# Self-attention on one core: the projection matmuls dealt out over the head slots

## What is computed

```python
x = x + attn(layernorm(x), w_qkv, w_out)      # 16 heads of 32, causal
x = x + xattn(layernorm(x), ctx, ctx, wq, wk, wv, wo)
x = x + ffn(layernorm(x), wg, W, b)           # top-1 of 8 experts
# attn: q, k, v = split(x @ w_qkv); p = softmax(mask(q k^T / sqrt(32))); (p v) @ w_out
```

## Time and profile before

| | us |
|---|---|
| median of 3 runs | 864.57 (862.69 to 866.25) |
| the profiled execution, its time | 868.03 |
| its span, first to last instruction | 866.3 |
| self-attention: S of head 0 of batch 0, last store issued | 29.26, 392.90 |
| one batch of 16 slots, in the middle | 44.13 |

### The profile page before, as it was taken

The page is one execution under the profiler, slowest core; times in us unless marked ns, Lnnn a source line. Parts: engine busy times, 40 slices in busy tenths (PEclk is TensorE's granted clock), DMA queues, the critical chain, the costliest instruction groups (busy, mean ns, idle before and its releaser), DMA issues. The chain is left out here.

```text
span 866.3 us, 19948 instructions
## 1 busy us (share of the span) xinstructions
PE 762.7 (88%) x6424; PEld 688.1 (79%) x6425; DVE 529.1 (61%) x1557; ACT 370.4 (43%) x1145; POOL 312.2 (36%) x456
## 2 busy tenths in 40 slices
PE   4798989898989999757999999999999985739995
PEld 4787979888888888646899998989899974637884
DVE  4678685868686867546565655556464533834664
ACT  4476675757575767534423232313133220622221
POOL 3376574757565656641000101010101101124662
PEclk9999999999999999879999999999999997868998
DMA  9643343444444434306712425060502111765630
GB/s 345 147 114 94 105 101 106 93 118 93 116 93 118 93 94 115 101 1 208 286 52 72 99 23 113 8 121 20 101 30 67 59 15 49 168 163 152 199 122 24
DMA packets 49575, 90.90 MB, mean 105 GB/s; under 512 B 11390, under 2 KB 11518, under 8 KB 49408
## 3 DMA queue, kind: packets, MB, share of 16 engines
q1 hardware_dynamic: 43872, 77.80, 34.2%
q0 software_dynamic: 5664, 12.61, 4.7%
HBM read 51.95 MB, written 18.77 MB: 82 GB/s over the span
## 5 line engine op out<-in xcount | busy, mean ns | idle before, releaser
L398 ACT ACTIVATE prob<-prob,nmax 128x128 f32<-128x128 f32 (+1 forms) x256 | 114.5, 448 | 77.9 <-DVE nmax L576 77.9
L337 POOL TENSOR_TENSOR pt_part<-pt_rest,pt_part 128x384 bf16<-128x384 f32 x128 | 117.8, 921 | 10.2
L335 POOL CAST pt_part<-pt_rest 128x384 bf16<-128x384 f32 x128 | 67.4, 527 | 113.5 <-DVE pt_rest L585 112.1
L576 DVE CUSTOM_DVE_ANT_0 prob<-a_s,mask 128x128 f32<-128x128 f32 (+1 forms) x256 | 80.2, 350 | 4.1 <-PE a_s L457 3.2
L585 DVE TENSOR_TENSOR pt_rest<-a_t,pt_part 128x384 f32<-128x384 f32 x128 | 70.8, 553 | 7.2 <-ACT pt_part L408 7.0
L408 ACT CAST pt_part<-a_t 128x384 bf16<-128x384 f32 x128 | 60.6, 473 | 32.3 <-PE a_t L470 32.1
L470 PE MATMUL a_t<-ident,prob 128*128 128x128 f32 x384 | 63.5, 275 | 12.2 <-DVE pt_rest L585 11.8
L457 PE MATMUL a_s<-stack 96*128 96x256 f32 x256 | 61.8, 324 | 0.2 <-DVE nmax L576 0.2
L470 PEld LDWEIGHTS a_t<-ident,prob 128*128 128x128 f32 x384 | 45.2, 141 | 17.9 <-issue 15.3
L488 PE MATMUL a_o<-pt_part,v_part 128*32 128x256 bf16 (+1 forms) x1536 | 40.4, 258 | 14.2 <-POOL pt_part L337 13.9
L922 ACT CAST b_kt_hi<-b_bank 128x256 fp32r<-128x256 f32 (+1 forms) x48 | 20.5, 445 | 66.1 <-PE b_bank L56 65.2
(11 more groups left out here) (217 smaller groups left out, 1986.1 us busy)
## 6 DMA issues: line engine op xcount, KB each, us to landing
stack<-qk SPq DMA_DIRECT2D x192, 128.0 KB, 2.4
stage<-in_w SPq DMA_DIRECT2D x8, 1024.0 KB, 8.9
xin<-in_x SPq DMA_DIRECT2D x8, 512.0 KB, 3.6
xr<-in_x SPq DMA_DIRECT2D x8, 512.0 KB, 3.6
x<-xr SPq DMA_DIRECT2D x8, 512.0 KB, 2.8
xin<-x SPq DMA_DIRECT2D x8, 512.0 KB, 8.9
b_cin<-in_ctx SPq DMA_DIRECT2D x8, 512.0 KB, 3.5
xr<-x SPq DMA_DIRECT2D x8, 512.0 KB
```

Source lines behind the costliest of these rows:

```text
L335: nc.gpsimd.tensor_copy(pt_part[1][:, t % NPT, :], rest).then_inc(pt_mid_done, 1)
L337: nc.gpsimd.tensor_tensor(pt_part[2][:, t % NPT, :], rest, pt_part[1][:, t % NPT, :], ALU.subtract).then_inc(pt_done, 1)
L398: a = nc.scalar.activation(prob[:, e % NPROB, cols], prob[:, e % NPROB, cols], ACT.Exp, scale=-1.0, bias=nmax[:, e, q:q + 1], accum_out=rs ...
L576: m = nc.vector.tensor_tensor_reduce(out=prob[:, s % NPROB, cols], in0=s_ps[s % 2][:, q, 0:P * (q + 1)], in1=mask[:, P * (1 - q):], scale= ...
```

## The change

Each job's matmuls may now be cut over neighbouring slots: PLAN gives, for every job, how many of its matmuls stand in which slot, and EARLY and FINISH say in which slot ACT and DVE evacuate it, near the slot's start or at its end (slot 16 is slot 0 of the next batch). k2, u0 and u1 become jobs of the batch itself and leave the prologue. In a slot, PE now does T before AV and the jobs. The stack copies go group by group: four times 12 DMAs of 64 KB in a batch, each group behind its own k job (k0 stands in slot 13 and is evacuated in slot 14), and PE waits once for all 12 of a group, at the group's first head. The broadcast copy of the reciprocal sums goes from DVE to POOL; the layer norm's steps are spread over slots 0 to 5; the tiles `r_sb` and `o_sb` get memory of their own, and the copy to `r_sb` comes one slot later. The core of the diff:

```diff
-def three_pass(pe_matmul, out, lhs, rhs, first=True, last=True):
+def three_pass(pe_matmul, out, lhs, rhs, begin=0, end=None):
...
-        ins = pe_matmul(out, a, b, start=first and i == 0, stop=last and i == len(steps) - 1)
+    for i in range(begin, len(steps) if end is None else end):
...
-        stack = sb("stack", [3 * HD, 2, HG, 2, GH, S], F32R)
+        stack = sb("stack", [3 * HD, G, HG, 2, S], F32R)
...
-        SLOTS = {0: ["q3"], 2: ["k3"], 4: ["w0"], 5: ["w1", "X0"], 6: ["X1"], 7: ["y0"], 8: ["y1"], 9: ["q0"], 10: ["k0"],
-                 11: ["q1", "k1"], 12: ["u0"], 13: ["u1"], 14: ["q2"], 15: ["k2"]}
-        OWN, LATE = ("q3", "k3", "w0", "w1"), ("y0", "y1")
-        ORDER = [j for s in sorted(SLOTS) for j in SLOTS[s]]
-        PROLOGUE = ["X0", "X1", "q0", "k0", "q1", "k1", "q2", "k2", "u0", "u1"]
+
+
+        PLAN = {"k2": {0: 2, 1: 10}, "q3": {1: 6, 2: 6}, "k3": {2: 10, 3: 2}, "u0": {3: 12}, "u1": {4: 2, 5: 10},
+                "w0": {5: 6, 6: 6}, "w1": {6: 12}, "X0": {7: 4}, "y0": {7: 5, 8: 1, 9: 6}, "X1": {9: 4},
+                "y1": {10: 8, 11: 4}, "q0": {11: 8, 12: 2, 13: 2}, "k0": {13: 12}, "q1": {14: 12}, "k1": {14: 6, 15: 6},
+                "q2": {15: 12}}
+
+        EARLY = {2: ["k2"], 4: ["u0"], 6: ["u1"], 7: ["w1"], 10: ["X1"], 14: ["k0"], 15: ["q1"], 16: ["q2"]}
+        FINISH = {2: ["q3"], 3: ["k3"], 6: ["w0"], 7: ["X0"], 9: ["y0"], 11: ["y1"], 13: ["q0"], 15: ["k1"]}
+        OWN, LATE = ("k2", "q3", "k3", "u0", "u1", "w0", "w1"), ("y0", "y1")
+        ORDER = list(PLAN)
+        PROLOGUE = ["X0", "X1", "q0", "k0", "q1", "k1", "q2"]
         assert sorted(PROLOGUE) == sorted(j for j in ORDER if j not in OWN + LATE)
         JOBS, HI_JOBS = len(ORDER), len(ORDER) - len(LATE)
         assert JOBS % 2 == 0
 
 
-        T_LAG, LO_LAG, RINV_LAG, AV_LAG, R_LAG, ON_LAG, OT_LAG = 2, 3, 3, 5, 5, 6, 7
-        LO_JOB_LAG = 1
+        T_LAG, LO_LAG, RINV_LAG, AV_LAG, ON_LAG = 2, 3, 3, 5, 6
+
+        OT_LAG = {9: (0,), 7: (1, 2, 3)}
 
         PASSES = ((0, 0), (1, 0), (0, 1), (1, 1), (2, 0), (0, 2))
-        EPILOGUE_SLOTS = 10
+        EPILOGUE_SLOTS = 13
         SPLIT_AT = {"X0": 0, "q0": 1, "q2": 2}
+        STATS_AT, AGGR_AT, RSTD_AT, APPLY_AT = (0, 1), 3, 3, (4, 5)
...
+        def parts_at(slot, n):
+
+            return [(j, sum(m for s, m in at.items() if s < slot), at[slot]) for j, at in PLAN.items()
+                    if slot in at and has(j, n)]
+
+        def leaving(table, slot, n):
+
+            jobs = [(j, n) for j in table.get(slot, []) if has(j, n)]
+            if slot == 0 and not (isinstance(n, int) and n == 0):
+                jobs += [(j, n - 1) for j in table.get(H, []) if has(j, n - 1 if isinstance(n, int) else n)]
+            return jobs
+
...
-            def stack_half(half):
+            def stack_group(g, n, early):
+
+                wait(sp, job_ev, job_at(f"k{g}", n) + 1)
+                sp.sem_inc(tick_sp, 1)
+                wait(sp, s_done, early)
                 for j in range(HG):
                     for r, parts in enumerate((slice(0, 3, 2), slice(1, 3), slice(0, 4, 3))):
-                        dst = stack[HD * r:HD * (r + 1), half, j, :, :, :].bitcast(F32)
-                        src = qk[HD * j:HD * (j + 1), half, parts, :, :].bitcast(F32)
-                        sp.dma_start(dst.rearrange("p w g s -> p w (g s)"),
-                                     src.rearrange("p w g s -> p w (g s)")).then_inc(stacked[half][j], 16)
+                        sp.dma_start(stack[HD * r:HD * (r + 1), g, j, :, :].bitcast(F32),
+                                     qk[HD * j:HD * (j + 1), g // GH, parts, g % GH, :].bitcast(F32))\
+                            .then_inc(stacked[g], 16)
 
             def batch(n):
 
-                wait(sp, job_ev, job_at("k3", n) + 1)
-                sp.sem_inc(tick_sp, 1)
                 if isinstance(n, int) and n == 0:
                     sp.wait_ge(w_split, 3)
+                stack_group(2, n, n * H - HG)
+                if isinstance(n, int) and n == 0:
                     sp.wait_ge(wo_split, 2)
-                wait(sp, s_done, n * H)
-                stack_half(1)
+                stack_group(3, n, n * H)
...
                 if has("k1", n):
-                    wait(sp, job_ev, job_at("k1", n) + 1)
-                    sp.sem_inc(tick_sp, 1)
-                    wait(sp, s_done, n * H + H // 2)
-                    stack_half(0)
+                    stack_group(0, n, n * H + HG)
+                    stack_group(1, n, n * H + 2 * HG)
 
             sp.wait_ge(xn_ready, TB)
             sp.dma_start(xin[:], batch_rows(x, 1)).then_inc(x_in, 16)
             sp.dma_start(xr[:], batch_rows(x, 0)).then_inc(xr_in, 16)
-            wait(sp, job_ev, job_at("k1", -1) + 1)
+            sp.wait_ge(w_split, 1)
+            stack_group(0, -1, 0)
             sp.wait_ge(w_split, 2)
-            stack_half(0)
...
+                g = group_at(h, RINV_LAG, n)
+                if g is not None:
+                    before = groups_before(h, RINV_LAG, n)
+                    pool.wait_ge(rinv8_done, before + 1)
+                    pool.sem_inc(tick_pool, 1)
+                    wait(pool, r_done, before)
+                    pool.sem_inc(tick_pool, 1)
+                    nc.gpsimd.tensor_copy(rinv[:], free_ap(rinv8[:, g, :, :], 0, [[HG, TB], [1, HG], [0, HD]]))\
+                        .then_inc(rinv_done, 1)
...
+            def job(j, n, begin=0, matmuls=None):
+
+                if begin == 0:
+                    if j == "X0":
+                        pe.wait_ge(xn_ready, (n + 2) * TB)
+                    if j == "q0":
+                        pe.wait_ge(job_ev, job_at("X1", n) + 1)
+                    if j == "u0" and isinstance(n, int) and n == 0:
+                        pe.wait_ge(w_split, 3)
+                    if j == "y0":
+                        pe.wait_ge(ot_done, n * G)
+                    wait(pe, job_ev, job_at(j, n) - 1)
+                pe_job(j, n, begin, matmuls)
...
-                    if s % (H // 2) < HG:
-                        pe.wait_ge(stacked[g // GH][j], (n + 1) * HEAD_IN)
+                    if j == 0:
+                        pe.wait_ge(stacked[g], (n + 1) * GROUP_IN)
                     wait(pe, mx_done, n * H + h - 1)
                     for q in range(TB):
-                        m = nc.tensor.matmul(s_ps[s % 2][:, q, :], stack[:, g // GH, j, 0, g % GH, q * P:(q + 1) * P],
-                                             stack[:, g // GH, j, 1, g % GH, :], start=True, stop=True)
+                        m = nc.tensor.matmul(s_ps[s % 2][:, q, :], stack[:, g, j, 0, q * P:(q + 1) * P],
+                                             stack[:, g, j, 1, :], start=True, stop=True)
                     m.then_inc(s_done, 1)
-                g = group_at(h, AV_LAG, n)
-                if g is not None:
-                    heads_by_values(g, h, n)
-                for j in jobs_of(h, n):
-                    job(j, n)
                 t = head_at(h, T_LAG, n)
                 if t is not None:
                     pe.wait_ge(ex_done, n * H + h - T_LAG + 1)
@@ -469,12 +503,17 @@
                     for o, cols in ((0, slice(2 * P, 3 * P)), (P, slice(0, P)), (2 * P, slice(P, 2 * P))):
                         m = nc.tensor.transpose(t_ps[t % 2][:, o:o + P], prob[:, t % NPROB, cols], ident[:])
                     m.then_inc(t_done, 1)
+                g = group_at(h, AV_LAG, n)
+                if g is not None:
+                    heads_by_values(g, h, n)
+                for j, begin, matmuls in parts_at(h, n):
+                    job(j, n, begin, matmuls)
...
-                before = h - LO_JOB_LAG
-                for j in jobs_of(before, n) if before >= 0 else jobs_of(H + before, n - 1 if isinstance(n, int) else n):
-                    of = n if before >= 0 else n - 1
-                    if isinstance(of, int) and of < 0:
-                        continue
-                    if j in LATE:
-                        dve.wait_ge(job_done, job_at(j, of) + 1)
-                        dve.wait_ge(xr_in, 16 * of)
-                        xt = xr[:, int(j[1]), :]
-                        nc.vector.tensor_tensor(xt, bank(j, of)[:, :], xt, ALU.add).then_inc(job_ev, 1)
-                    else:
-                        evac(j, of)
...
-                    dve.wait_ge(rinv8_done, before + 1)
-                    wait(dve, ot_done, before)
-                    nc.vector.tensor_copy(rinv[:], free_ap(rinv8[:, g, :, :], 0, [[HG, TB], [1, HG], [0, HD]]))\
-                        .then_inc(rinv_done, 1)
...
+                    if j in LATE:
+                        dve.wait_ge(job_done, job_at(j, of) + 1)
+                        dve.wait_ge(xr_in, 16 * of)
+                        xt = xr[:, int(j[1]), :]
+                        nc.vector.tensor_tensor(xt, bank(j, of)[:, :], xt, ALU.add).then_inc(job_ev, 1)
+                    else:
+                        evac(j, of)
```

(58 more changed lines are left out.)

89 lines of the change are left out of this document (42 added, 47 removed).

## The result

| | before | changed |
|---|---|---|
| median, us | 863.96 (862.69 to 866.25, 4 runs) | 900.75 (898.65 to 902.52, 4 runs) |
| ratio, 95% interval | | 1.0427 (1.0397 to 1.0458) |
| profiled execution, its span | 868.03, 866.3 | 898.65, 896.9 |
| S of head 0 of batch 0; last store of the stage | 29.26; 392.90 | 28.41; 428.97 |

The change makes the kernel 36.8 us slower, where 23.5 were forecast. 900.75 lies inside the range of 862 to 905, but above the 880 to 897 that the prediction gave its own case. The loss is in self-attention: its last store is issued 36.1 us later. The spans differ by 30.6 only, because the last stage of the profiled execution happened to be 5.7 us shorter; nothing there was changed.

The account below looks back on a forecast made before the run. PE was taken to bound self-attention, with 4.9 us of stalls a batch. Start and batch 0 +5.4, batches 1 to 6 +20.7 and batch 7 -2.6 gave +23.5 us on 864.6: 888.1 us, range 862 to 905.

Parts of the forecast that it names:

- its own case: Whole kernel: the forecast by its own terms, 880 to 897 us, likeliest 888.1; chance 0.54.
- The bound and the stalls: Self-attention, middle batch of 44.13 us: PE bounds it with 39.2 us of work, plus 4.9 us of stalls.
- The old stalls: PE waits in a middle batch, such as 1.1 us on the split of T; balanced slots would remove them.
- The stack copies: Top of each batch: twelve DMAs land 11.4 us after slot 14 starts; PE has 5.24 us of work, waits 6.2.
- rivals by bytes: Stack DMA issue on SP goes by bytes, 0.345 us each: 862 us, 849 if the clock stays up; chance 0.13.
- by the price of the x load: Stack DMA issue on SP costs 0.39 + 0.045 us, between the other prices: 870 us; chance 0.08.
- Two of the prediction's signs: Middle batches: S of heads 0 spaced 47 to 49 us; one PE wait on stack copies of 5.5 to 7 us.
- The start of the first S: Start of batch 0: S of head 0 starts at 28.6 us instead of 29.26, after twelve issues and the last landing.
- The waits of the jobs: Slots 2, 6 and 7: k3, w1 and y0 wait for evacuations, 1.0 us a batch together, ends 0 and 2.
- The clock: After each stack wait PE runs at half rate for a stretch, losing 1.6 us, ends 0 and 4.0.
- The sum: Middle batch: 34.0 + 1.0 + 11.4 + 1.6 = 48.0 us instead of 44.13; whole kernel +23.5 us.
- Smaller edits: Broadcast copy on POOL at about 0.5 us, spread layer norm and later r_sb copy: no cost; job waits 1.0 us.

Follow-up runs that it names:

- evacuations first: Changed kernel with a semaphore per head, four buffers for v_rest, and DVE taking EARLY evacuations ahead of the maxima: 831.09 us, ratio 0.9602 to the kernel before.
- whole jobs: Changed kernel with semaphore per head, four v_rest buffers and EARLY evacuations ahead of the maxima, but every job whole in one slot: 849.13 us, ratio 0.973.
- The filler run: Changed kernel with 40 additional matmuls of 256 columns ahead of the stack copy wait in slot 0 of batches 1 to 7: 885.21 us, ratio 1.0242.
- six copies awaited: Changed kernel with a semaphore per head, S of heads 0 and 2 of a group waiting for two heads' six DMAs: 856.9 us, ratio 0.9916.
- evacuations first and one wait for twelve: Changed kernel with its one wait for twelve copies, four v_rest buffers and EARLY evacuations ahead of the maxima: 886.25 us, ratio 1.0244.

## Why the prediction was right, and what was mis-sized

- **The bound and the stalls.** Right. PE's sum of 39.2 us a batch was the floor that evacuations first came to within 0.8 us of. The old stalls on the split of T went with the balance: they are not among the waits of a middle batch of the changed kernel, and with whole jobs they came back as 2.8 us.
- **The stack copies.** Right, step by step: SP starts 1.83 us into slot 14; the price of an issue did not fall with the bytes (median 597 ns for 64 KB, 603 for 128 KB in the earlier trace rows), so the rivals by bytes and by the price of the x load are out. Landing fell to 2.0 us, and slots 14 and 15 with the wait take 11.0 us instead of 11.4. Two of the prediction's signs missed all the same. The wait itself is 4.7 us and not 5.5 to 7: PE's own work in the two slots is stretched by job waits from 5.24 to 6.3 us, which the prediction put inside the stack wait and did not take off it, and landing is 0.4 shorter. And batches are 49.0 to 50.2 us apart, not 47 to 49. The start of the first S came out near by luck. The terms 18.15 + 0.15 + 7.1 + 2.4 + 0.1 give 27.9 us, not the 28.6 written; in the changed kernel the first copy is issued at 19.1, 0.8 later than taken, landing is 0.4 shorter, and S starts at 28.4.
- **The waits of the jobs.** Mis-sized: 1.0 us a batch was taken, with 2 as the upper end; slots 0 to 13 without the clock's part show 2.4. From the changed kernel, DVE's maxima in slot 2, then slots 2, 6, 7 and 10, then the first slots of two batches:

```profile
229.44 0.29 DVE L609 CUSTOM_DVE_ANT_0 prob<-a_s,mask 128x128 f32<-128x128 f32 x1 [0.42 <-PE a_s L496]
...
228.82:231.74 2.92, 2.70 (x24) 2.50 (x22) 2.44 (x10) 2.10 (x8) 1.53 (x3) 1.00 0.00 0
238.97:242.14 3.17, 2.94 (x25) 2.74 (x24) 2.63 (x10) 2.12 (x8) 2.46 (x5) 1.00 0.41 100
242.14:245.59 3.45, 2.44 (x17) 1.98 (x16) 2.19 (x7) 2.30 (x7) 3.29 (x7) 1.00 0.42 103
250.46:253.03 2.57, 2.57 (x17) 2.20 (x16) 2.36 (x8) 2.04 (x6) 1.02 (x2) 1.00 0.00 0
...
271.27:275.43 4.16, 4.16 (x60) 3.27 (x61) 2.04 (x7) 1.40 (x6) 1.40 (x2) 0.61 0.44 108
221.28:226.12 4.84, 4.84 (x59) 3.92 (x60) 2.04 (x7) 1.55 (x6) 1.42 (x2) 0.50 0.43 106
```

Slot 2 (228.82) is 0.52 above its sum, slot 6 (238.97) 0.48, slot 7 (242.14) 1.26. For the first two the times in the prediction were right (0.5 and 0.4), but I then cut the 1.6 of the three waits to 1.0, because I took DVE to be late in the slot of the earlier trace rows. That was the mistake: in slot 2 DVE had stood idle for 0.42 us and still began the maxima only 0.62 after S, so nearly all of the 0.70 is S itself. In slot 7 POOL's part was not seen at all: the prediction counted the evacuation of w1 that y0 waits for, and left out what DVE itself waits for before it.
- **The clock.** Right in kind, too small in size. The first slot of the batch at 221.28 ran wholly at 0.50, 4.84 us against a sum of 2.54; the next batch's, from 271.27, at 0.61 and 4.16. With the slot behind it that is a loss of 2.6 and 1.6 us in turn, where 1.6 was taken for all. The filler run puts the seven waits between batches at 15.5 us, 2.2 each, where the sum had 7 x 1.6 = 11.2. The two stretches at half rate, with PE idle in the first 1.3 us of the long one:

```profile
219.94:226.74 6.80, 5.46 (x62) 4.56 (x63) 2.04 (x7) 1.73 (x6) 1.42 (x2) 0.50 0.41 101
271.15:274.55 3.40, 3.28 (x53) 2.49 (x53) 2.04 (x7) 1.36 (x5) 0.52 (x2) 0.50 0.42 104
```

- **The sum.** 34.0 + 2.4 + 11.0 + 2.2 = 49.6 us for a middle batch, measured 49.7, forecast 48.0: the job waits were 1.4 us too small, the clock 0.6, and the copies 0.4 too large. Batches 1 to 6 hold 10.4 of the 12.6 us that were missing in the stage; batch 0 holds 2.3. Its clock loss was covered by the 1.6 of the sum (slots 0 and 1 are 1.2 over); what was missing are waits on DVE and ACT behind light slots, for which 1.3 to 1.6 us a slot had been taken. The two longest, in slots 8 and 11:

```profile
48.40 0.52 PE L504 MATMUL a_t<-ident,prob 128*128 128x128 f32 x3 [1.38 <-DVE pt_rest L620]
...
54.59 0.52 PE L504 MATMUL a_t<-ident,prob 128*128 128x128 f32 x3 [1.45 <-ACT prob L450]
```

- **Smaller edits.** The copy on POOL takes 0.4 us and is not waited for; nothing to correct.

## What to carry to other kernels

Price the work that a schedule does not show as waiting: SP's copies never appeared among PE's waits, but they had 8.7 us of lead. A plan that evens out PE by moving their producer, so that 3.4 us of PE's work are left ahead of their use (5.24 - 1.83), puts 12 issues of 0.6 us on the path. Ask of each moved step what must follow it before its user can start, and let the user wait for its own part only. When a wait of several microseconds on PE comes into a loop, add the clock behind it, and when jobs share buffers, follow the wait through every engine that holds the buffer.

## What the runs showed of the hardware

- An SBUF to SBUF DMA on 32 partitions costs SP 0.60 us to issue, the same for 64 and 128 KB; a load of 512 KB from memory cost 0.39.
- A single wait of PE of 1.0 us left the granted clock at 1.00 (six copies awaited), and so did waits of up to 0.9 us spread over a middle batch of the kernel before. But in batch 1 of that kernel three waits of 0.56, 0.84 and 0.85 us fell within 4.2 us, in which PE was busy half of the time, and the clock then was 0.50 for 3.2 us:

```profile
71.15 0.52 PE L470 MATMUL a_t<-ident,prob 128*128 128x128 f32 x3 [0.56 <-DVE pt_rest L585]
...
72.74 0.52 PE L470 MATMUL a_t<-ident,prob 128*128 128x128 f32 x3 [0.84 <-DVE pt_rest L585]
...
74.36 2.11 PE L488 MATMUL a_o<-pt_part,v_part 128*32 128x256 bf16 x48 [0.85 <-POOL pt_part L337]
...
70.00:74.20 4.20, 2.11 (x16) 1.56 (x14) 4.01 (x15) 3.17 (x12) 3.16 (x5) 0.98 0.01 2
74.20:77.40 3.20, 3.04 (x53) 2.46 (x53) 2.81 (x13) 1.44 (x6) 0.86 (x3) 0.50 0.20 44
```

- A wait of 4.7 us brought a stretch at 0.50 of 3.4 or of 6.8 us, in turn from batch to batch in the middle of the changed kernel, beginning at most 1.4 us before PE resumed. The length of the wait does not decide which: with a wait of 4.62 us it was 6.8 every time in the kernel with evacuations first and one wait for twelve.
- 40 matmuls in each of seven such waits, whose result nobody reads, made the changed kernel 15.5 us faster.
